# Expert biases as full-width rows added by VectorE, the normalising pass on ScalarE, and no bias matmul

## What is computed

```python
def reference(x, ctx_2048, mask_BxS2_bk0, g_xattn, g_ffn, Wg, W, b):
    # x: 32 x 112 x 512, ctx: 32 x 375 x 512, W: 8 x 512 x 512, b: 8 x 512, all float32
    xn = layernorm(x)
    attn = softmax(where(mask, xn @ ctx.T / sqrt(512), -1e30))
    x = x + tanh(g_xattn) * (attn @ ctx)              # attention with the context as keys and values
    r = layernorm(x)
    probs = softmax(r @ Wg); idx = argmax(probs)      # one expert of eight for each row
    x = x + tanh(g_ffn) * probs[idx] * (r @ W[idx] + b[idx])
    return x
```

## Time and profile before

| | |
|---|---|
| times of the runs | 398.06, 399.58, 400.54 us; median 399.58 us |
| profiled execution, its own time | 398.33 us |
| its span, first to last instruction | 396.4 us |
| PE busy | 360.9 us, 91% of the span |
| VectorE, ScalarE, GpSimd busy | 292.1, 192.8, 223.7 us |
| granted TensorE clock, mean over the span | 0.988 |

### The profile page before, as it was taken

One profiled execution on the slowest core, in us unless ns is written; L12 is line 12 of the kernel. 1 busy time (PEld: TensorE's weight loads), 2 busy tenths in 40 slices (PEclk: granted clock), 3 DMA queues, 4 the chain that ended last, 5 costly groups with the idle time before them and its releaser, 6 DMA issues.

```text
span 396.4 us, 9462 instructions
## 1 busy us (share of the span) xinstructions
PE 360.9 (91%) x2037; PEld 300.4 (76%) x2048; DVE 292.1 (74%) x1089; ACT 192.8 (49%) x453; POOL 223.7 (56%) x456
## 2 busy tenths in 40 slices
PE   0879999999999999999999999668999999999980
PEld 0768888888888888888888877456777777777760
DVE  2467889889889888889889989476775666655540
ACT  2267777777777676777777766221111111111100
POOL 8323656656656665666566554745566555556520
PEclk9999999999999999999999999989999999999996
DMA  6586787778878888889888872325544544444400
GB/s 167 150 207 167 188 221 201 200 210 201 204 218 200 184 225 197 204 194 209 207 213 189 217 198 69 84 54 133 154 143 142 156 138 125 145 145 138 153 30 0
DMA packets 39237, 65.20 MB, mean 164 GB/s; under 512 B 11306, under 2 KB 11918, under 8 KB 39216
## 3 DMA queue, kind: packets, MB, share of 16 engines
q1 hardware_dynamic: 32592, 48.38, 50.6%
q0 software_dynamic: 6624, 16.58, 13.7%
HBM read 49.62 MB, written 17.12 MB: 168 GB/s over the span
## 4 chain that ended last, share of the span: by engine, by line
PE 79%; DMA 7%; DVE 4%; issue 4%; SPq 2%; ACT 1%; POOL 1%; POOLq 0%; DVEq 0%; ACTq 0%
PE read_both L1132 10%; PE ctx_ps L1076 9%; PE read_both L1133 9%; PE score_ps L1171 8%; PE score_ps L1173 8%; PE score_ps L1172 8%; PE score_ps L1101 4%; PE ctx_ps L1153 4%; PE score_ps L1098 3%; PE score_ps L1099 3%; PE score_ps L1100 3%; DMA ctx_sb<-in_ctx 3%; PE prob_ps L1085 3%; DMA ctx_sb<-mid_rows,take 2%; PE prob_ps L1111 2%
## 5 line engine op out<-in xcount | busy, mean ns | idle before, releaser
L646 ACT ACTIVATE ctxT_hi<-ctx_ps 128x512 fp32r<-128x512 f32 x35 | 21.0, 599 | 102.3 <-PE ctx_ps L1153 102.3
L1132 PE MATMUL read_both<-ctx_sb 125*112 125x264 f32 x192 | 61.1, 400 | 2.0 <-DVE lg L828 1.7
L521 POOL DMA_INDIRECT token_list<-pay,pos x32 | 32.3, 1010 | 50.8 <-DVE pos L880 46.1
L1171 PE MATMUL score_ps<-w_hi,ctxT_hi 128*128 x140 | 58.8, 420 | 1.6 <-DVE ctxT_lo L899 1.6
L960 DVE TENSOR_TENSOR ctxT_lo<-ctx_ps,ctxT_hi 128x375 fp32r<-128x375 f32 x96 | 49.4, 542 | 13.2 <-ACT ctxT_hi L638 12.9
L1076 PE MATMUL ctx_ps<-ident,ctx_sb 125*128 125x125 f32 x384 | 54.2, 278 | 3.8 <-DVE ctxT_lo L960 2.1
L1133 PE MATMUL read_both<-ctx_sb 125*112 125x256 f32 x192 | 57.1, 379 | 0.0
L1173 PE MATMUL score_ps<-w_lo,ctxT_hi 128*128 x140 | 55.7, 398 | 0.0
L1172 PE MATMUL score_ps<-w_hi,ctxT_lo 128*128 x140 | 55.1, 394 | 0.0
L591 POOL DMA_INDIRECT ctx_sb<-mid_rows,take x35 | 34.6, 990 | 36.0 <-DVE ctx_sb L918 32.8
L918 DVE SCALAR_TENSOR_TENSOR ctx_sb<-score_ps,li,ctx_sb 128x512 f32<-128x512 f32 x35 | 26.3, 750 | 32.2 <-PE score_ps L1174 23.7
(11 more groups left out here) (143 smaller groups left out, 785.9 us busy)
## 6 DMA issues: line engine op xcount, KB each, us to landing
ctx_sb<-in_ctx SPq DMA_DIRECT2D x32, 672.0 KB
w_raw<-in_L_ffn_W SPq DMA_DIRECT2D x32, 256.0 KB, 5.0
x_sb<-in_x SPq DMA_DIRECT2D x32, 224.0 KB, 4.1
mid_rows<-x SPq DMA_DIRECT2D x32, 224.0 KB, 3.2
ctx_sb<-in_ctx SPq DMA_DIRECT2D x32, 78.0 KB
li<-token_list SPq DMA_DIRECT2D x35, 2.0 KB, 1.8
ctx_sb<-mid_rows,take POOLq DMA_INDIRECT x35, 3.5
out_rows<-ctx_sb,put POOLq DMA_INDIRECT x35, 2.9
```

The lines of the kernel that those rows point to most:

```text
L1132: pe.matmul(read_a, turned[:, 0:S], turned[:, S:SE + HALF], start=(c == 0), stop=(c == MC - 1))
L1171: pe.matmul(y_ps[a][:, :], hi, w_hi[:, chunk], start=(k == 0), stop=False)
```

## The change

1. The bias matmul, its operands `b_pick`, `b_rows` and `b_part`, and the code that made them in the first 27 us (memsets and selects on POOL, a split on DVE, four transfers on SP) are gone.
2. The eight bias rows are loaded late, each broadcast to all 128 partitions (256 KB each), into the context slots that batches 28 to 30 have left (`biases`). SP issues them among the last batches. The gathered rows now go into the ring of `x_sb` in place of a piece of the context ring, so the first four gathers wait for `x2_ok` (the batch's new rows are made) in place of `read_mm`.
3. The normalising of a tile's rows goes from DVE to ACT (`normal`), as one `Identity` activation with scale and bias; POOL's record holds minus mean times reciprocal deviation in place of the mean, which is one more small POOL instruction for each batch.
4. DVE has a new step for each tile, ahead of the last one: it reads the tile's expert from memory into a register and adds scale times bias row to the gathered rows, in place. The last step waits for it.

```diff
 # SP, behind the loads of the first four pieces of the list
+            def load_bias(e):
+                sp.dma_start(biases[:, e, :], b_exp[e:e + 1, :].to_broadcast([P, D])).then_inc(b_ld, 16)
+
+            sp.wait_ge(read_mm, B - 3)
+            for e in range(0, MC):
+                load_bias(e)
...
+            batch(Count(B - 2))
...
 # POOL, gather(t)
-                    pool.wait_ge(read_mm, B - 3 + t.at)
+                    pool.wait_ge(x2_ok, B - 3 + t.at)
 # ACT
+            def normal(t):
+                act.wait_ge(row_ld[t.slot(4)], t.rounds(4) * 16 + 16)
+                if t.at_least(2):
+                    act.wait_ge(rnT_mm, t.times(1, -1))
+                else:
+                    act.wait_ge(w_lo_ok, B - 1 + t.at)
+                act.activation(rn[:, t.slot(2), :], rows[:, t.slot(4), :], ACT.Identity,
+                               bias=li[:, bass.ds(t.times(1), 1), 3:4].rearrange("p o c -> p (o c)"),
+                               scale=li[:, bass.ds(t.times(1), 1), 2:3].rearrange("p o c -> p (o c)")).then_inc(rn_ok, 1)
+
             def tile(t):
+                turned_rows(t)
+                if t.plus(1).within(TILES):
+                    normal(t.plus(1))
 # DVE, tile(i)
-                    dve.tensor_scalar(rn[:, t.slot(2), :], rows[:, t.slot(4), :],
...
+                    if t.turn is None and t.at == 0:
+                        dve.wait_ge(b_ld, 16 * E)
+                        dve.wait_ge(early_map_ok, 2)
+                    expert = dve.value_load(tile_expert[0:1, bass.ds(t.times(1), 1)], min_val=0, max_val=E - 1)
+                    dve.scalar_tensor_tensor(rows[:, b, :], biases[:, bass.ds(expert, 1), :].rearrange("p o d -> p (o d)"),
+                                             li[:, bass.ds(t.times(1), 1), 1:2].rearrange("p o c -> p (o c)"),
+                                             rows[:, b, :], ALU.mult, ALU.add).then_inc(base_ok, 1)
+                    dve.wait_ge(base_ok, t.times(1, 1))
                     dve.wait_ge(y_mm, t.times(1, 1))
 # PE, products(t)
-                    pe.matmul(y_ps[a][:, :], b_pick[:, bass.ds(expert, 1), :].rearrange("q o p -> q (o p)"), b_rows[:, :],
-                              start=False, stop=True).then_inc(y_mm, 1)
```

More of the change, by code:

```diff
@@ L182, in build @@
         wg_mid = sb("wg_mid", [P, KC, E])
-        b_part = [sb(f"b_part{i}", [E * KC, P], BF16) for i in range(3)]
-        b_rows = sb("b_rows", [P, D], BF16)
         mask_row = sb("mask_row", [P, 4, M], BF16)
@@ L202, in build @@
         x2 = sb("x2", [S, 2, D])
-        b_raw, b_rest = x2[0:E * KC, 1, 0:P], [x2[0:E * KC, 1, (i + 1) * P:(i + 2) * P] for i in range(2)]
         st1 = sb("st1", [S, 2, 6])
@@ L255, in build @@
         put = sb("put", [P, 4], U32)
-        rows, res = ctx_sb[:, 0:4, 0, SE:], ctx_sb[:, 0:4, 1, SE:]
+        rows, biases, res = x_sb, ctx_sb[:, 0:E, SE:], ctx_sb[:, E:E + 4, SE:]
         rn = w_raw
@@ L435, in _ @@
                 load_list(Count(t))
-            for i in range(B - 2, B):
-                batch(Count(i))
+            def load_bias(e):
[3 more added lines that the diff above has]
+                load_bias(e)
+            sp.wait_ge(read_mm, B - 2)
+            for e in range(MC, 2 * MC):
+                load_bias(e)
+            batch(Count(B - 2))
+            sp.wait_ge(read_mm, B - 1)
+            for e in range(2 * MC, E):
+                load_bias(e)
+            batch(Count(B - 1))
             for t in range(4, EARLY):
@@ L519, in file @@
                 pool.wait_ge(scale_ok, now)
+                pool.wait_ge(nm2_ok, now)
                 filing.begin(j)
@@ L686, in apply1 @@
                     act.wait_ge(xnT_mm, j.times(1))
-                act.activation(xn[:, :], x_sb[:, j.slot(4), :], ACT.Identity, bias=ln1[:, a, 1:2],
+                act.activation(xn[:, :], x_sb[0:S, j.slot(4), :], ACT.Identity, bias=ln1[:, a, 1:2],
                                scale=ln1[:, a, 0:1]).then_inc(xn_ok, 1)
@@ L693, in batch @@
                 if at in (B, B + 1):
-                    tile(Count(0 if at == B else 2))
+                    turned_rows(Count(0 if at == B else 2))
+                    normal(Count(1 if at == B else 3))
                 if at == B - 2:
@@ L713, in batch @@
                 if at == B:
-                    tile(Count(1))
+                    turned_rows(Count(1))
+                    normal(Count(2))
                 if soon.within(B):
```

94 lines of the change are left out of this document (34 added, 60 removed).

## The result

| | before | after |
|---|---|---|
| median of 20 runs each | 399.7 us | 397.02 us |
| range of the runs | 398.06 to 401.78 | 394.7 to 400.5 |
| profiled execution, own time (span) | 398.33 (396.4) | 396.76 (394.9) |

The ratio is 0.9935, with a 95% interval of 0.9916 to 0.9953. The prediction was 394.0 us, a gain of 5.5; the gain is 2.7. The time lies in the range of 391.4 to 399.5, but the size is off by a factor of two.

A forecast was written before the change was run, and what follows sets the result against it. PE was taken to bound the tiles, busy 92.52 of 93.00 us. 7.6 - 0.5 - 0.7 - 0.6 - 0.3 = 5.5 us gained, so 399.58 - 5.5, about 394.0 us; range 391.4 to 399.5 us.

The forecast's parts named there:

- The bias matmul, 7.6 us: On PE, tiles 2 to 34 each lose a matmul of 0.23 us: 33 x 0.23 = 7.6 us gained.
- DVE in a tile: DVE's round with register load (0 to 0.6 us) and addition (0.75) is 2.92 us, under PE's 3.21.
- The rival that DVE sets the pace: In the tiles, an uncovered load and waits make DVE's round 3.3 to 3.4 us: 396 to 399.5 us; chance 0.20.
- The lock behind POOL's issues: Rival: in each tile the addition waits for POOL's gather or scatter issue: 400 or 441 us; slow form's chance 0.06.
- The row of 0.85 us: Trace row before the change: a DVE step on eight numbers lasted 0.85 us, ending with POOL's subtraction.
- The entry, 1.2 us: Between attention and tiles: ACT's slower normalising, twice, costs 0.5 us; bias loads delay the first gather by 0.7.
- The rival that the bias loads stop DVE at tile 0: At the entry, bias loads at 100 GB/s land at 273, DVE stands 6 us: 397 to 398 us; chance 0.14.
- Tiles 3 to 7 and the ring, 0.6 + 0.3 us: Later map lengthens DVE's round in five tiles, 0.6 us lost; gathers have 0.2 us slack over two rounds, 0.3 lost.

The follow-up runs named there:

- the two traces of after: The changed kernel unchanged, profiled twice: first measurement ratio 0.9935 to the kernel before, the repeat as control 0.9916.
- the run with a shorter ring: Changed kernel, but the addition writes into the output slot and the gather waits for the addition, not the last step; ratio 0.9871 to the kernel before.
- all four variants that keep its order and ScalarE's pass: Changed kernel with the old record on POOL (ratio 0.9900), without bias loads (0.9902), without the addition (0.9908), or with gathers waiting for the addition (0.9871).
- the late cast: Changed kernel with gathers waiting for the addition, gathers of tiles 3 and 0 early, and DVE casting tile t+4's row numbers after tile t's addition; 394.13 us, ratio 0.9753.

## Why the prediction was half right

- **The bias matmul, 7.6 us: right for each tile.** 3.43 us a tile became 3.20 (3.21 forecast). Tiles 3 to 34 are 31 x 0.23 = 7.1 us shorter where nothing waits, the rest lies behind tile 34 (0.40 us measured). Taken out alone it brought 6.4 us, since waits came up that the longer round had covered.
- **DVE in a tile: right.** The addition has 0.75 us, the load 0.33 in the tile shown (between my 0 and 0.6), and from tile 12 on the addition costs nothing. The rival that DVE sets the pace does not hold. With the normalising pass left on DVE the tiles come 3.64 us apart, but by DVE's wait for gathers, not by its work.
- **The lock behind POOL's issues: did not happen.** On the page, 35 additions have a mean of 754 ns, and POOL issued a gather during the one shown; in the two traces of after the longest has 0.82 us. The row of 0.85 us that spoke for the lock is a step with one tensor operand, not two. The rule of the Trainium skill on two SBUF inputs ("SBUF — State Buffer", Who interferes with whom), which the prediction weighed, does not show with POOL's indirect transfers here.
- **The entry, 1.2 us: 1.85 measured.** Both terms were right in size: ScalarE's pass 0.27 us twice, the bias loads 0.7 to 0.9 us on the first gather. The rest is POOL's multiplication, 0.17 us where I took nothing, and the first transposes at 1.2 GHz, 0.45 us. These add up to about 1.9 us, but by rows alone: without the loads the entry was 27.97 us and without the multiplication 28.08, so no run confirms the split. The rival that the bias loads stop DVE at tile 0 did not come: its addition started at 270.43 without a wait for them.
- **Tiles 3 to 7 and the ring, 0.6 + 0.3 us: the step that failed.** In tiles 3 to 34 the two traces of after are 2.5 and 4.4 us over PE's pace, those of before 0.5 and 0.3 us over theirs: a loss of 3.1 us by the means, against the 0.9. I had the mechanism of the ring, with 0.2 us of slack, and sized it as a rare accident; but a tile that is late is never made good, since PE has no faster pace to catch up with. Tiles 12 to 34 lost 0.85 to 0.96 us that way, and the run with a shorter ring got 0.9 of it back. Two parts I did not see at all. One is the wait for the list of tile 12, 0.7 to 1.2 us, whose row is in the trace of before and which goes with the late cast: I costed the later map as busy time on DVE (0.72 us a tile) and left out the load that hangs on its end. The other is the clock: in one of the two traces of after, and in all four variants that keep its order and ScalarE's pass, 1.6 us are lost behind tile 3. This loss did not come in the three runs of the change with the gather of tile 3 early, where PE stood idle for only 0.41 to 0.52 us. I costed the delay of the gather of tile 3, not the slow products behind PE's longer idle time. By the run of before without the bias matmul, 1.6 us more than in the traces of before are lost in tiles 3 to 34 from the shorter round alone, without the addition or ScalarE's pass.
- **A slip in the sum:** from its own terms the bounds come out as 391.7 and 397.7 us, not 391.4 and 397.5. Nothing above hangs on it.

What stays open: why the first transposes kept 2.4 GHz in one trace with 3.30 us of idle time before them; how often the slow products behind tile 3 come over many executions (the 20 runs of after spread over 5.8 us, those of before over 3.7); and the losses between tiles 4 and 11, from 0.3 us with the shorter ring to 1.5 us with the late cast, of which 1.4 are a gap of 4.58 us ahead of tile 6. There POOL issues the gather of tile 6 behind the scatter of batch 31's records, 1.9 us after the addition that frees its slot was through (277.38), and the rows are slow to come, 5.08 us from issue to ACT's pass (DVE, POOL and ACT in that kernel's timeline); no run parts the order on POOL from the slow transfer:

```profile
276.60 0.78 DVE L926 SCALAR_TENSOR_TENSOR ctx_sb<-ctx_sb,li,x_sb 128x512 f32<-128x512 f32 x1
...
277.98 0.96 POOL L530 DMA_INDIRECT token_list<-pay,pos  x1 [0.30 <-issue]
279.24 0.97 POOL L598 DMA_INDIRECT x_sb<-mid_rows,take  x1 [0.30 <-issue]
...
284.32 0.81 ACT L654 ACTIVATE w_raw<-x_sb,li 128x512 f32<-128x512 f32 x1 [2.48 <-DMA x_sb<-mid_rows,take]
```

## What to carry to other kernels

When the bounding engine gets shorter, list every wait that its old period covered, not only the engines' busy time: each transfer that an in-order engine stands at, with the instructions queued behind it, and above all those that free a buffer for the next transfer. A ring with 0.2 us to spare at the median loses at every slow landing and gains nothing back, so give it slack first (here by freeing the gathered rows one step earlier); and look behind a wait that idles the matmul engine as well: here 1.6 us at the lower clock followed in five traces of six. Keep the wait for a gather off the engine whose later steps free the slot for the next gather: the same change gained 2.7 us with the normalising pass on ScalarE and lost 5 with it on VectorE.

## What the hardware showed that was not expected

- A register load on DVE is read ahead of the vector instruction that runs: with 0.30 to 0.60 us of its own (median 0.51) and 0.19 us of register steps behind it, it showed as 0.38 us of idle time a tile in the profile after.
- DVE's step with two SBUF operands takes as long as the one with a PSUM operand (medians of 752 and 751 ns in the profile after), also during POOL's issue of a gather.
- POOL issues a gather 0.83 us after the last step has ended where it waited for it inside its loop, and 0.27 us for the gathers of tiles 32 to 34, which are unrolled behind the loop, in the traces of after.
